# TensorE returns a group's seven 0/1 matrix slots in three signals instead of seven, and the histogram operands get a second buffer

## What is computed

```python
h = batch_norm(layernorm(x) @ w1.T + b1, g1, bt1)          # 6250 x 256
m = segment_max(h[src] - h[dst], dst, num_segments=6250)   # over 200000 edges
m = where(isfinite(m), m, 0)
hg = gelu(batch_norm(concat([h, m]) @ wg.T + bg, gg, btg))
x = x + batch_norm(hg @ w2.T + b2, g2, bt2) + layernorm(x)
# then eight experts, each three matrix products, weighted by a softmax
x = x + layernorm(x) + sum_e w_e * (relu(bn(relu(bn(y @ W1_e)) @ W2_e)) @ Wo_e + bo_e)
```

## Time and profile before

| | |
|---|---|
| median of 3 runs | 3649.25 us (3648.39 to 3667.12) |
| span of the profiled execution, first to last instruction | 3634.8 us |
| PE busy | 2966.5 us, 82% |
| DVE busy | 2207.0 us, 61% |
| ACT busy | 1962.2 us, 54% |
| POOL busy | 1496.1 us, 41% |
| mean granted TensorE clock | 0.905 |

### The profile page before, as it was taken

The page is one execution under the profiler, slowest core; times in us unless marked ns, Lnnn a source line. Parts: engine busy times, 40 slices in busy tenths (PEclk is TensorE's granted clock), DMA queues, the critical chain, the costliest instruction groups (busy, mean ns, idle before and its releaser), DMA issues. The chain is left out here.

```text
span 3634.8 us, 41575 instructions
## 1 busy us (share of the span) xinstructions
PE 2966.5 (82%) x15504; PEld 2461.7 (68%) x15504; DVE 2207.0 (61%) x4089; ACT 1962.2 (54%) x2741; POOL 1496.1 (41%) x1530
## 2 busy tenths in 40 slices
PE   6578777787877778788887777728988999999998
PEld 5456565665665656566665666527878999999998
DVE  6576666666666666666666666540885556555544
ACT  5356555555555655555555555415165565566554
POOL 1566565565666655556665555561410000000000
PEclk9789898898898998889898898868999999999999
DMA  7355555555555555455555555450213324333331
GB/s 227 114 195 196 181 197 187 194 197 182 194 191 189 189 169 170 167 169 181 170 183 169 171 176 171 160 204 25 61 75 98 118 105 135 128 115 115 115 109 69
DMA packets 164927, 559.97 MB, mean 154 GB/s; under 512 B 31190, under 2 KB 68374, under 8 KB 157556
## 3 DMA queue, kind: packets, MB, share of 16 engines
q1 hardware_dynamic: 87492, 355.23, 26.1%
q0 software_dynamic: 77232, 202.08, 19.5%
HBM read 320.19 MB, written 237.00 MB: 153 GB/s over the span
## 5 line engine op out<-in xcount | busy, mean ns | idle before, releaser
L648 POOL DMA_INDIRECT ring<-runs,src_i x1436 | 1410.4, 982 | 1004.2 <-DVE ring L815 518.7
L999 PE MATMUL ps<-oh,zhl 128*128 128x512 f32 x3136 | 1347.5, 430 | 321.9 <-issue 159.7
L1001 PE MATMUL ps<-oh,zhl 128*128 128x512 f32 x3136 | 1308.0, 417 | 12.8 <-issue 12.5
L670 ACT ACTIVATE oh<-ids,nodeneg 128x512 fp32r<-128x512 f32 x896 | 633.6, 717 | 900.7 <-PE ps L1001 487.4
L999 PEld LDWEIGHTS ps<-oh,zhl 128*128 128x128 f32 x3136 | 642.1, 205 | 515.2 <-issue 186.4
L815 DVE SCALAR_TENSOR_TENSOR ring<-ring,pen 128x256 f32<-128x256 f32 x1564 | 750.4, 480 | 63.5 <-DMA ring<-runs,src_i 32.3
L821 DVE TENSOR_SCALAR oh<-ps,nodef 128x512 fp32r<-128x512 f32 x672 | 501.7, 747 | 403.6 <-PE ps L1001 248.5
L1001 PEld LDWEIGHTS ps<-oh,zhl 128*128 128x128 f32 x3136 | 643.2, 205 | 146.1 <-issue 15.3
L675 ACT ACTIVATE oh<-oh,ones 128x512 fp32r<-128x512 f32 x896 | 613.6, 709 | 0.0
L827 DVE TENSOR_TENSOR oh_lo<-lo,ps 128x896 bf16<-128x896 bf16 x224 | 242.8, 1084 | 328.7 <-remote 302.3
L1569 ACT ACTIVATE av<-ps,vecs 128x896 f32<-128x896 f32 x224 | 246.3, 1100 | 330.4 <-PE ps L191 330.4
(11 more groups left out here) (294 smaller groups left out, 3872.2 us busy)
## 6 DMA issues: line engine op xcount, KB each, us to landing
runs<-ring SPq DMA_DIRECT2D x136, 896.0 KB
fw<-wsp SPq DMA_DIRECT2D x56, 1536.0 KB, 6.5
runs<-ring SPq DMA_DIRECT2D x102, 768.0 KB
ring<-runs,src_i POOLq DMA_INDIRECT x1436
ids<-srcT_d SPq DMA_DIRECT2D x32, 256.0 KB
res_d<-x_all SPq DMA_DIRECT2D x7, 896.0 KB
y<-res_d SPq DMA_DIRECT2D x7, 896.0 KB, 7.0
part<-in_Wx SPq DMA_DIRECT2D x16, 384.0 KB
```

The source lines that it names most:

```text
L648: pool.indirect_dma_start(ring[:, k, :], None, runs[0:N, :], bass.IndirectOffsetOnAxis(ap=src_i[:, STEPS * i + k:STEPS * i + k + 1], axis= ...
L670: act.activation(oh[:, v, :], ids[:, bass.ds(h, 1), :].rearrange("p a n -> p (a n)"), ACT.Abs, bias=nodeneg[:, bass.ds(SLOTS * g + v, 1)]) ...
L999: pe.matmul(ps[:, two + k, :], z_hi(g)[:, v, cols], oh[:, v, :], start=g == 0 and v == 0, stop=False, skip_group_check=True)
L1001: r = pe.matmul(ps[:, two + k, :], z_lo(g)[:, v, cols], oh[:, v, :], start=False, stop=False, skip_group_check=True)
```

## The change

PE raises `s_ohf` three times in a group: after slot 1 (for slots 0 and 1), after slot 3 (for 2 and 3) and after slot 6 (for 4, 5 and 6). The waits of ACT and DVE are renumbered to match (`freed`). `oh_lo` and `oh_hi` exist twice and are used in turn; the second pair lies behind the ring. The signal `s_cnt` is gone. Before it overwrites a pair, DVE waits for the first `s_ohf` signal of the group before (PE runs the counts of a group ahead of its slots, so that signal covers the older counts). Which instructions compute, and in which order, stays as it was on every engine.

```diff
--- before.py
+++ after.py
@@ -55,6 +55,8 @@
 LEAD = 21
 BD = (1, 3, 5)
 BA = (0, 2, 4, 6)
+PART = (0, 0, 1, 1, 2, 2, 2)
+NPART = 3
 
 GM = 4
 LASTW = E - (P - 1) * WIN
@@ -272,8 +274,10 @@
                  ("nodeneg", NT * 4), ("fixi", 64), ("tri", P * 4), ("ones", P * 4))
         lo16 = plan.at("lo16", [P, HR * HCOL], BF16, p2["lo16"])
         hi16 = plan.at("hi16", [P, HR * HCOL], BF16, p2["hi16"])
-        oh_lo = plan.at("oh_lo", [P, NG, P], BF16, p2["oh_lo"])
-        oh_hi = plan.at("oh_hi", [P, NG, NT], BF16, p2["oh_hi"])
+        spot = places["zT"] + STEPS * C * 4
+        oh_lo = [plan.at(f"oh_lo{j}", [P, NG, P], BF16, at) for j, at in enumerate((p2["oh_lo"], spot))]
+        oh_hi = [plan.at(f"oh_hi{j}", [P, NG, NT], BF16, at) for j, at in enumerate((p2["oh_hi"], spot + NG * P * 2))]
+        assert spot + NG * P * 2 + NG * NT * 2 <= places["zT"] + MAT
         iota = plan.at("iota_i", [P, P], I32, places["part_hi"])
         io_lo, io_hi = ps[:, 1, 0:P], ps[:, 1, P:P + NT]
         tri = plan.at("tri", [P, P], F32, p2["tri"])
@@ -630,6 +634,10 @@
 
             return GS[g] - (NPE if g == NG - 1 and 1 <= i <= PG else 0)
 
+        def freed(i, g, v):
+
+            return NPART * (NG * i + g) + PART[v] + 1
+
         def gathered(i, g):
 
             return 16 * sum(by_pool(j, g) for j in range(i + 1))
@@ -666,7 +674,7 @@
                     act.activation(ring[:, PSLOT:STEPS, :].rearrange("p s n -> p (s n)"), banks(two, 2), ACT.Copy).then_inc(s_pe, 1)
 
                 def distance(i, h, g, v):
-                    wait(act, s_ohf, NT * i + SLOTS * g + v + 1)
+                    wait(act, s_ohf, freed(i, g, v))
                     act.activation(oh[:, v, :], ids[:, bass.ds(h, 1), :].rearrange("p a n -> p (a n)"), ACT.Abs,
                                    bias=nodeneg[:, bass.ds(SLOTS * g + v, 1)]).then_inc(s_ab, 1)
 
@@ -817,19 +825,21 @@
                                              op0=ALU.add, op1=ALU.max).then_inc(s_ch, 1)
 
                 def one_hot(i, h, g, v):
-                    wait(dve, s_ohf, NT * i + SLOTS * g + v + 1)
+                    wait(dve, s_ohf, freed(i, g, v))
                     dve.tensor_scalar(oh[:, v, :], ps[:, bass.ds(6 + h, 1), :].rearrange("p a n -> p (a n)"),
                                       nodef[:, SLOTS * g + v:SLOTS * g + v + 1], None, ALU.is_equal).then_inc(s_ohd, 1)
 
                 def low_hots(i, g):
-                    wait(dve, s_cnt, NG * i + g + 1)
+                    t = NG * i + g + 1
+                    if t >= 2:
+                        wait(dve, s_ohf, NPART * (t - 1) + 1)
                     at = HCOL * i + g * NG
-                    dve.tensor_tensor(oh_lo[:], lo16[:, bass.ds(at, NG)].unsqueeze(2).to_broadcast([P, NG, P]),
+                    dve.tensor_tensor(oh_lo[t % 2][:], lo16[:, bass.ds(at, NG)].unsqueeze(2).to_broadcast([P, NG, P]),
                                       io_lo.unsqueeze(1).to_broadcast([P, NG, P]), ALU.is_equal)
 
                 def high_hots(i, g):
                     at = HCOL * i + g * NG
-                    dve.tensor_tensor(oh_hi[:], hi16[:, bass.ds(at, NG)].unsqueeze(2).to_broadcast([P, NG, NT]),
+                    dve.tensor_tensor(oh_hi[(NG * i + g + 1) % 2][:], hi16[:, bass.ds(at, NG)].unsqueeze(2).to_broadcast([P, NG, NT]),
                                       io_hi.unsqueeze(1).to_broadcast([P, NG, NT]), ALU.is_equal).then_inc(s_oh, 1)
 
                 def low(i):
@@ -890,8 +900,8 @@
 
                 dve.tensor_copy(srcf[:].rearrange("p (g s) -> p g s", s=NPE),
                                 src_i[:, STEPS:STEPS * (PG + 1)].rearrange("p (g s) -> p g s", s=STEPS)[:, :, PSLOT:STEPS]).then_inc(s_srcf, 1)
-                dve.memset(oh_lo[:], 0.0)
-                dve.memset(oh_hi[:], 0.0).then_inc(s_oh, 1)
+                dve.memset(oh_lo[0][:], 0.0)
+                dve.memset(oh_hi[0][:], 0.0).then_inc(s_oh, 1)
                 dve.tensor_copy(nodef[:], node_i[:])
                 dve.tensor_copy(io_lo, iota[:])
                 dve.tensor_copy(io_hi, iota[:, 0:NT])
@@ -967,8 +977,7 @@
 
                     wait(pe, s_oh, t + 1)
                     for n in range(NG):
-                        r = pe.matmul(ps[:, 0, 0:NT], oh_lo[:, n, :], oh_hi[:, n, :], start=False, stop=False, skip_group_check=True)
-                    r.then_inc(s_cnt, 1)
+                        pe.matmul(ps[:, 0, 0:NT], oh_lo[t % 2][:, n, :], oh_hi[t % 2][:, n, :], start=False, stop=False, skip_group_check=True)
 
                 def turn_back(i):
 
@@ -1000,7 +1009,8 @@
                                           skip_group_check=True)
                                 r = pe.matmul(ps[:, two + k, :], z_lo(g)[:, v, cols], oh[:, v, :], start=False,
                                               stop=False, skip_group_check=True)
-                            r.then_inc(s_ohf, 1)
+                            if v == SLOTS - 1 or PART[v + 1] != PART[v]:
+                                r.then_inc(s_ohf, 1)
                         if g == 1 and i:
                             turn_back(i - 1)
                     for k in range(KC):
@@ -1010,7 +1020,7 @@
                 pe.wait_ge(s_srcf, 1)
                 pe.transpose(ps[:, 6, 0:P], srcf[:], ident[:]).then_inc(s_srcT, 1)
                 pe.matmul(ps[:, 0, 0:NT], zr[:], zr[:, 0:NT], start=True, stop=False, skip_group_check=True)
-                pe.sem_inc(s_ohf, SLOTS)
+                pe.sem_inc(s_ohf, NPART)
                 for c in range(NCH):
                     for m in range(KC):
                         for j, (a, w) in enumerate(PIECES):
```

## The result

The change makes the kernel slower. Median 3707.8 us (3702.2 to 3709.5, 4 runs) against 3648.8 us in the same group of runs; ratio 1.0161, 95% interval 1.0134 to 1.0188. The profiled execution spans 3700.5 us, 65.7 more than that of the earlier trace rows.

A forecast was written before the change was run, and what follows sets the result against it. Picking was taken as bound by POOL's gathers plus chain waits from held PE signals; only fewer POOL waits gained, 149 us, other terms 0: 3634.8 - 149 = 3485.8 us span, plus 14.5 gives 3500 us, range 3340 to 3640.

The forecast's parts named there:

- What bounds the kernel: Picking, 2192 of 3634.8 us: PE's signals are held while POOL gathers without pause, so POOL waits 498 us for the chain.
- POOL's 1694 us: Picking stretch: the least POOL makes it cost, 2192 us less the 498 us it waits for the chain.
- A signal's own price: PE's matmuls: sending a signal costs 0; the skill's 26 ns each would have made the gain 29 us.
- The hold, 149 us: Picking: 2.9 signals still pass per run, now freeing 6.2 slots; POOL waits fall from 170 to 119, saving 149 us.
- Rival A: Pending signals fill the path, one POOL wait per 10.9 signals: 299 us saved, 3350 us; chance 0.18.
- rival B: The hold is untouched, POOL's run length alone decides and each cycle moves one group: 3649 us; chance 0.13.
- No `s_cnt`: DVE's 302.3 us wait at `oh_lo` goes but moves to slot 1 of the next group; alone worth 0.
- Later release, put at 0: Slots return 0.9 or 1.8 us later to ACT and DVE; with 0.85 us of delay free, cost 0.
- rival C: Coarse release makes PE wait for slot 2 where signals are over 0.85 us late: 97 us lost, 3746 us; chance 0.07.
- the ladder of the earlier trace: Picking, inside a gather run: ACT and DVE, each waiting for the next slot, start one at a time, 2.13 us apart.
- the hold of the earlier trace: Picking, gather run from 1389.05 us: late signals arrive together after POOL stops, the counts' signal 7.4 us late.
- After a release nothing is saved: PE's first slot then waits for ACT's two distances and one_hot 0, as long as the dropped `oh_lo`, chain, `oh_hi`.

The follow-up runs named there:

- e3: The kernel before with POOL's gathers left out after the first of 34 rounds: 2898.3 us, one execution.
- e12: The kernel before with three small memsets on POOL after each gather: 3422.0 us, ratio 0.9527 to the kernel before.
- e16: The changed kernel with seven slot signals a group and ACT's one_hot 0 and 2 right behind their distances: 3078.2 us, ratio 0.9998 to the kernel before.
- e4: The changed kernel with POOL's gathers left out after the first round: 2904.9 us, one execution.
- e13: The changed kernel with three small memsets after each gather and one wait of POOL on them per group: 3414.4 us, ratio 1.1096 to the kernel before.
- e14: The kernel before with three small memsets after each gather and one wait of POOL on them per group: 3410.8 us, ratio 1.1078 to the kernel before.
- e1: The changed kernel with a signal for each slot, seven a group (second operand pair kept, no s_cnt): 3649.7 us, ratio 1.0068 to the kernel before.
- e2: The kernel before with only the three slot signals a group (one operand pair, s_cnt kept): 3665.8 us, ratio 1.0115 to the kernel before.
- e9: The changed kernel with ACT's one_hot 0 and 2 moved right behind their distances: 3590.0 us, ratio 1.0011 to the kernel before.
- e10: The kernel before with ACT's one_hot 0 and 2 moved right behind their distances: 3561.9 us, ratio 0.9907 to the kernel before.
- e8: The kernel before with each gather after the first round bringing 128 of 256 columns: 3578.2 us against 3591.4, one execution.
- e7: The kernel before with POOL at most 13 steps ahead of the chain instead of 21: 3601.6 us, ratio 1.0009 to the kernel before.
- e17: The kernel before with two small memsets after each gather: 3242.0 us, ratio 1.053 to the kernel before.
- e18: The kernel before with two small memsets after each gather and ACT's one_hot 0 and 2 right behind their distances: 3243.7 us, ratio 1.0531 to the kernel before.
- e5: The kernel before with a drain on POOL after every gather: 6454.5 us, ratio 1.7942 to the kernel before.
- e11: The kernel before with one small memset on POOL after each gather: 3646.3 us, ratio 1.0148 to the kernel before.

## Why the prediction was wrong, point by point

*What bounds the kernel.* Right. The time above POOL's 1694 us is made of PE signals that are held while POOL gathers closely. e3, with no gathers, lets PE run at its own 47.9 us a round; e12, with gathers 1.49 us apart, has no holds; e16, at 1740 us of picking, comes within 50 us of the floor.

*A signal's own price.* Put at 0, and the pair without gathers agrees: with 1120 signals fewer, e4 took 6.6 us more than e3, in one execution each, and e13 took 3.6 us more than e14. The estimate from the Trainium skill, page "TensorE: Matmul & The Clock Gate", section "The cost: per-tile semaphore tail", was 29 us less; no run shows it here.

*The hold, 149 us.* This is the step that failed. It took 2.9 signals to come through in each cycle whatever they stand for, so that 13.2 slots would move per wait of POOL. In the same reckoning the changed kernel has 736 signals in 215 waits, 3.4 a wait. Three of them are a group's, so only 0.4 would have come through, and 1568 / 215 = 7.3 slots moved, fewer than the 9.2 of before. The wait count did not fall to 119 but rose from 170, and the time in these waits from 498 to 575 us. The number of signals that pass in a run is no constant. The table in the section on the result shows what decides: a signal sent in the first 6 us of a run is prompt (0.91 and 0.83), one sent after 9 us is not (0.07 and 0.05), with seven signals a group as with three. In those first 6 us PE sends 560 signals before and 265 after, so that few come through because few are sent, and no slots are gained. Nor do more slots fall into the hold: the signal that covers a slot is sent over 6 us into a run for 0.51 of the slots before and 0.47 after. Rival A, a path filled by the number of signals, is wrong for the same reason; rival B was nearer. The reading that all held signals come "at once a little after POOL stops" was too simple as well. Of the waits over 1.5 us late about half ended while POOL was still gathering, in both kernels (181 of 375, and 184 of 398). Nor is a wait a cycle: picking has 142 runs of gathers for its 170 waits before, and 160 for 215 after.

*No `s_cnt`.* The wait moved, as said: 302.3 + 248.5 + 132.6 us became 716 us at the slots. That this is worth 0 was wrong by the 25 us of e1. Through which step it costs them is open; e1 with ACT's order fitted (e16) fell where there are no holds.

*Later release, put at 0.* The second term that was wrong, and named as rival C with a chance of 0.07. The three signals alone cost 41 us (e2) where nothing was allowed for. The place was right (PE waits for slot 2, because one_hot 2 stands behind the wait for slot 4), and slot 0 belongs to it as well, since one_hot 0 stands behind the wait for part 2. The point from which it decides was right too: prompt signals hide it (e4, e13), held ones don't. But the step that C names is not all of it. C's 97 us stand against 20 to 31 us that go with the fitted order; 28 us of the change's 59 stay in e9 against e10 without a shown step. I rejected C because "such groups wait longer today, for more signals in a row". That holds for the ladder of the earlier trace rows but not for the hold of the earlier trace rows, where the trace has seven slot signals between 1406.04 and 1406.39, so that seven cost hardly more than one. Of the 1372 signals of `s_ohf` that the trace of before has, 342 come within 0.1 us of the one ahead of them.

*After a release nothing is saved.* PE's idle time at the counts fell by 98 us and at slot 4 by 75, and it rose at slots 0 and 2 by 246.

## What to carry to other kernels

When a signal is late, find out what it is late with before making signals fewer: here the delay came from another engine's work, and what paid was to put three small memsets between that engine's gathers (e12, 4.7% faster under holds), or to let nothing stand behind the late signal (e10, 0.9%). When a repair is tried on the changed kernel, try it on the kernel before as well: e9 alone looked like a full repair, e10 beside it shows that it was not. Order a producer's instructions so that none waits behind a signal it does not need. A fix for a contention has to be timed both with and without it: with e12's memsets the kernel is 11% slower where the holds are absent (e14), while e9's and e10's reordering lost nothing in any run.

## What the runs showed of the hardware that I had not expected

- While POOL issued indirect gathers 1.26 us apart, PE's signals came late, by up to 17.8 us in picking and 23 us at its end, and in one hold PE's own small matmuls came in steps of 0.7 or 1.4 us. With three memsets between gathers, 1.49 us apart, this was gone (e12); with half the bytes it was not (e8).
- The same kernel on the same chip took 3591 us at one hour and 3080 us at another; the traces kept from that chip show the holds in the first (e7, e8) and none in the second (e17, e18, with gathers 1.36 us apart). e16, on another chip, has none at 1.26 us. No run shows what switches them.
- Where signals were held, the traces lack most of the increments that report a gather's landing: 4969 of 22976 are there in the kernel before, 22965 in e16. Whether recording causes the holds is open.
- A drain on POOL behind an indirect gather lasts until the gather has landed: that takes 2.8 us from its start, and the next one starts 0.77 us later, 3.5 us from gather to gather instead of 1.26 us (e5).
- A memset of one column on POOL takes 0.09 to 0.12 us and, once per gather, does not change the gathers' spacing (e11).
